# Column sums of cos·Q and sin·Q: from wide TensorE products to elementwise sums on VectorE

## The reference, cut to what matters

```
Q = relu(x @ Wq + bq)
V = x @ Wv + bv
Q = relu(layer_norm(Q))
H = sum(Q, axis=1) ** 2,  scaled by pi / (2 m)          # one angle for each node
cosQ, sinQ = Q * cos(H), Q * sin(H)
out  = cosQ @ (cosQ.T @ V) + sinQ @ (sinQ.T @ V)
norm = cosQ @ sum(cosQ, axis=0) + sinQ @ sum(sinQ, axis=0) + 1e-10
h    = out / norm + gcn(x) + V
result = layernorm(x + relu(layer_norm(h, gamma, beta)))
```

## Time and profile before

| | |
|---|---|
| Time, median of 3 runs | 1686.92 us |
| Profiled execution, its own time | 1702.43 us |
| Its span, first to last instruction | 1700.6 us |
| Mean granted TensorE clock | 0.977 of full speed |
| TensorE matmuls busy | 1529.1 us (90%) |
| VectorE busy | 1093.6 us (64%) |
| GpSimd busy | 916.2 us (54%) |
| ScalarE busy | 608.9 us (36%) |
| DMA moved | 423.89 MB, mean 249 GB/s |

### The profile page before, as it was taken

The page is one execution under the profiler, slowest core; times in us unless marked ns, Lnnn a source line. Parts: engine busy times, 40 slices in busy tenths (PEclk is TensorE's granted clock), DMA queues, the critical chain, the costliest instruction groups (busy, mean ns, idle before and its releaser), DMA issues.

```text
span 1700.6 us, 25340 instructions
## 1 busy us (share of the span) xinstructions
PE 1529.1 (90%) x7913; PEld 943.0 (55%) x7913; DVE 1093.6 (64%) x3318; ACT 608.9 (36%) x1384; POOL 916.2 (54%) x1026
## 2 busy tenths in 40 slices
PE   5788999899999997999998999889999999999994
PEld 3566777666555563443433433336666766666663
DVE  6999676676666666434445444447777768777774
ACT  5999875533233222111112111113333333333332
POOL 0000000166666766666676777666666666666662
PEclk9999999999999997999999999989999999999997
DMA  6444444598888888888888888879888888888884
GB/s 224 139 154 160 151 157 153 201 314 291 297 285 286 290 287 263 262 266 267 266 253 257 264 270 273 271 208 288 283 271 279 277 271 277 286 273 271 285 256 142
DMA packets 172759, 423.89 MB, mean 249 GB/s; under 512 B 24142, under 2 KB 25802, under 8 KB 172616
## 3 DMA queue, kind: packets, MB, share of 16 engines
q0 software_dynamic: 71120, 236.74, 45.5%
q1 hardware_dynamic: 79980, 146.16, 25.1%
q10 hardware_dynamic: 21516, 39.29, 6.1%
HBM read 351.42 MB, written 70.67 MB: 248 GB/s over the span
## 4 chain that ended last, share of the span: by engine, by line
PE 60%; issue 12%; DVE 10%; DMA 7%; POOL 4%; ACT 4%; another core or an unknown queue 1%; POOLq 0%; SPq 0%; DVEq 0%; ACTq 0%
PE bank L1382 13%; PE bank L1383 12%; PE bank L1384 12%; PE bank L1503 10%; PE bank L1505 9%; POOL gathered L566 4%; DMA gathered<-scaled_g,index_slots 3%; DVE stage L984 3%; DVE stage L980 2%; ACT stage L638 1%; DMA scaled_g<-pairs 1%; DVE operands L993 1%; ACT operands L617 1%; DMA combine<-values 1%
## 5 line engine op out<-in xcount | busy, mean ns | idle before, releaser
L566 POOL DMA_INDIRECT gathered<-scaled_g,index_slots x882 | 877.1, 994 | 418.1 <-issue 203.8
L1100 DVE TENSOR_SCALAR one_hot<-iota_bf,dst_in_tile,gathered 128x128 bf16<-128x128 bf16 x882 | 269.7, 327 | 373.8 <-DMA gathered<-scaled_g,index_slots 212.9
L1503 PE MATMUL bank<-gathered,one_hot 128*128 128x512 f16 x882 | 344.9, 391 | 77.0 <-issue 39.4
L1382 PE MATMUL bank<-weights,operands 128*128 128x512 f32 x784 | 398.4, 508 | 14.2 <-DVE stage L1000 4.4
L1505 PE MATMUL bank<-gathered,one_hot 128*128 128x512 f16 x882 | 339.6, 385 | 5.1 <-issue 4.6
L1383 PE MATMUL bank<-weights,operands 128*128 128x512 f32 x784 | 313.7, 400 | 1.8 <-issue 1.8
L1384 PE MATMUL bank<-weights,operands 128*128 128x512 f32 x784 | 312.6, 399 | 0.6 <-issue 0.6
L1503 PEld LDWEIGHTS bank<-gathered,one_hot 128*128 128x128 bf16 x882 | 85.5, 97 | 253.5 <-issue 163.5
L736 ACT ACTIVATE operands_f<-operands,cos_sin_v 128x512 f16<-128x512 f32 x98 | 70.2, 721 | 360.5 <-remote 171.2
L1382 PEld LDWEIGHTS bank<-weights,operands 128*128 128x128 f32 x784 | 150.7, 192 | 80.7 <-issue 7.6
L551 POOL COPY dst_slots<-dst_cols 128x18 f32 x49 | 12.7, 260 | 332.7 <-issue 331.2
(11 more groups left out here) (243 smaller groups left out, 2066.8 us busy)
## 6 DMA issues: line engine op xcount, KB each, us to landing
operands<-values SPq DMA_DIRECT2D x98, 256.0 KB
stage<-in_x SPq DMA_DIRECT2D x96, 256.0 KB, 2.7
turned_x<-operands SPq DMA_DIRECT2D x37, 512.0 KB, 3.3
operands<-turned_x SPq DMA_DIRECT2D x37, 512.0 KB
gathered<-scaled_g,index_slots POOLq DMA_INDIRECT x882
scaled_g<-pairs SPq DMA_DIRECT2D x49, 260.0 KB, 2.0
pairs<-scaled_g SPq DMA_DIRECT2D x49, 260.0 KB
values<-stage ACTq DMA_DIRECT2D x49, 256.0 KB
```

What stands on the lines that cost most here:

```text
L566: pool.indirect_dma_start(out=plain(row_ring[k % RING]), out_offset=None, in_=table, in_offset=bass.IndirectOffsetOnAxis(ap=index_slots[:, ...
L1100: dve.tensor_scalar(one_hot[:, k % HOT, :], iota_bf[:, :], column(dst_in_tile, seq % 2 * PER_TILE + k), scale_of(row), ALU.is_equal, ALU.m ...
L1382: pe.matmul(out_ap, a_hi, b_hi, start=start and n == 0, stop=False, skip_group_check=True)
L1503: pe.matmul(gcn_banks[seq % 2][:, :], one_hot[:, k % HOT, :], hi, start=k == 0, stop=False, skip_group_check=True)
```

## The change

TensorE's two wide products of each tile are taken out, with `cs_wide`, its high and low parts, and the product that cleared bank 7. In their place VectorE keeps two 128 x 512 float32 rooms, `angle_sums`, in two buffers of `pairs` that are free by then. They are zeroed before the cosine sweep, and in each sweep `add_half` does room = half of Q · cosine (or sine) + room for both halves of each tile: 98 instructions in the cosine sweep, and 98 in the sine sweep. At the end of each sweep TensorE turns the room into four columns with four small fp32 products against a column of ones (`turn_sums(sweep)`), and `split_sums(sweep)` makes four of the eight numbers at a time. So the sine sums come at the end of the sine sweep, and no longer at that of the cosine sweep.

```diff
-                act.activation(cs[:, :, 0:2], ..., ACT.Copy, scale=UP).then_inc(s["cs_rounded"], 1)
-                act.wait_ge(s["cs_split"], 1)
+                act.wait_ge(s["angles_scaled"], 1)
...
             def split_angles():
-                dve.wait_ge(s["cs_rounded"], 1)
-                dve.tensor_tensor(both_parts[:, :], ident[0:4, 0:2], ident[0:4, 2:4], ALU.add)
-                dve.tensor_scalar(cos_sin_v[:, :], cos_sin[:, :], v_factor, None, ALU.mult)
-                dve.scalar_tensor_tensor(cs[:, :, 2:4], pair, UP, cs[:, :, 0:2], ALU.mult, ALU.subtract)\
-                    .then_inc(s["cs_split"], 1)
+                dve.wait_ge(s["cos_sin_ready"], 1)
+                dve.tensor_scalar(cos_sin_v[:, :], cos_sin[:, :], v_factor, None, ALU.mult).then_inc(s["angles_scaled"], 1)
+                for room in angle_sums:
+                    dve.memset(room, 0.0).then_inc(s["sums_begun"], 1)
+
+            def add_half(sweep, t, half):
+                g, r, room = 2 * (sweep * TILES + t) + half, rows_of(t), angle_sums[sweep]
+                dve.wait_ge(s["sums_begun"], 2)
+                dve.wait_ge(s["sums_added"], g)
+                dve.scalar_tensor_tensor(room[0:r], halves(q_tile(t))[half][0:r], column(cos_sin, 2 * t + sweep)[0:r],
+                                         room[0:r], ALU.mult, ALU.add).then_inc(s["sums_added"], 1)
...
-            def split_sums():
+            def split_sums(sweep):
+                mine = moment_sums[:, 4 * sweep:4 * sweep + 4]
...
                 for t, at in in_flight(cos_at, TILES, q):        # VectorE
                     if at == 1:
                         m_split(2 + t)
+                    if at in (1, 2):
+                        add_half(0, t, at - 1)
...
-                if q == COS_END + 3:
-                    keep_sums()
                 if q == COS_END + 7:
-                    split_sums()
+                    split_sums(0)
...
+                    if at in (0, 2):                             # VectorE, sine sweep
+                        add_half(1, t, at // 2)
                 if q == SIN_END:
+                    split_sums(1)
                     take_sines(0)
                     take_sines(1)
...
-                    if sweep == 0 and b == 0:                    # TensorE, m_products
-                        pe.matmul(banks[7][:, :], angles, f[0], start=False, stop=False, ...)
-                    if sweep == 0 and b == 1:
-                        pe.matmul(banks[7][:, :], angles, f[1], start=False, stop=False, ...)
...
-            def turn_sums():
-                pe.wait_ge(s["sums_kept"], 1)
+            def turn_sums(sweep):
+                pe.wait_ge(s["sums_added"], 2 * TILES * (sweep + 1))
                 for b in range(B):
-                    last = pe.matmul(banks[2][:, 2 * b:2 * b + 2], sum_rows[:, b * P:(b + 1) * P], both_parts[:, :], ...)
+                    last = pe.matmul(sum_banks[sweep][:, b:b + 1], angle_sums[sweep][:, b * P:(b + 1) * P],
+                                     ones_column[:, :], start=True, stop=True)
...
-                if q == COS_END + 5:                             # TensorE
-                    turn_sums()
+                if q == COS_END + 3:
+                    turn_sums(0)
...
                 if q == SIN_END:
+                    turn_sums(1)
                     o_turn(0, 0)
```

More of the change, by code:

```diff
@@ L135, in build_layer @@
         sums = sb("sums", [P, B, 4], F32R)
-        cs_wide = sb("cs_wide", [P, 4 * (TILES - 1) + P], F16)
-        cs = cs_wide[:, 0:4 * TILES].rearrange("p (t c) -> p t c", c=4)
-        both_parts = sb("both_parts", [4, 2], F32)
+        ones_column = sb("ones_column", [P, 1], F32)
         bn_parts = sb("bn_parts", [P, 3, 6], F32)
@@ L146, in build_layer @@
         edge_banks = banks[6], banks[7], banks[0], banks[6]
-        sum_rows = pairs[0:4, 3, 0:D]
+        angle_sums = [pairs[:, 1 + sweep, 0:D] for sweep in range(2)]
+        sum_banks = banks[2], banks[7]
         turned_banks = banks[2], banks[7]
@@ L253, in build_layer @@
             "extra_ready", "gcn_summed", "v_summed", "spread_step", "extremes_turned",
[L254 removed]
+            "factor_spread", "o_split", "o_normed", "o_root1", "o_stats2",
             "o_root2", "variance_linked", "factors_linked", "norm_linked", "mix_linked",
@@ L846, in _ @@
             dve.reg_mov(extras_done, 0)
-            dve.memset(cs_wide[:, 4 * TILES:], 0.0)
+            dve.memset(ones_column[:, :], 1.0)
             dve.memset(ln_eps, LN_EPS).then_inc(s["ident_ready"], 1)
@@ L1194, in take_cosines @@
                 dve.tensor_copy(stage[:, 2 + b, :], banks[3 + b][:, :]).then_inc(s["cos_taken"], 1)
-            def keep_sums():
-                dve.tensor_copy(sum_rows, banks[7][0:4, :]).then_inc(s["sums_kept"], 1)
-            def split_sums():
+            def split_sums(sweep):
+                mine = moment_sums[:, 4 * sweep:4 * sweep + 4]
                 dve.wait_ge(s["rows_bias_loaded"], 32)
[L1201 to L1206, removed]
+                dve.wait_ge(s["sums_turned"], sweep + 1)
+                link(dve.tensor_scalar(mine, sum_banks[sweep][:, 0:4], 1.0 / (UP * UP), None, ALU.mult))
+                link(dve.tensor_copy(sums[:, :, sweep], mine))
+                link(dve.tensor_tensor(sums[:, :, 2 + sweep], mine, plain(sums[:, :, sweep]), ALU.subtract))
+                link(dve.tensor_scalar(mine, mine, moment_up, None, ALU.mult))
             def fix_cosines(b):
@@ L1210, in fix_cosines @@
                 dve.wait_ge(s["cos_taken_act"], 2)
-                dve.scalar_tensor_tensor(stage[:, 2 + b, :], bias[:, 1, :], moment_sums[:, 2 * b:2 * b + 1],
+                dve.scalar_tensor_tensor(stage[:, 2 + b, :], bias[:, 1, :], moment_sums[:, b:b + 1],
                                          stage[:, 2 + b, :], ALU.mult, ALU.add).then_inc(s["moment_fixed"], 1)
@@ L1216, in take_sines @@
                 dve.wait_ge(s["moment_split"], 4)
-                dve.scalar_tensor_tensor(stage[:, 2 + b, :], bias[:, 1, :], moment_sums[:, 2 * b + 1:2 * b + 2],
+                dve.scalar_tensor_tensor(stage[:, 2 + b, :], bias[:, 1, :], moment_sums[:, 4 + b:5 + b],
                                          banks[3 + b][:, :], ALU.mult, ALU.add).then_inc(s["moment_fixed"], 1)
@@ L1585, in m_begin @@
                     pe.wait_ge(s["late_paired"], done(FUSED - 1))
-                    pe.wait_ge(s["cs_split"], 1)
                 pe.wait_ge(s["m_split"], done(sweep * TILES))
-                if sweep == 0:
-                    pe.matmul(banks[7][:, :], zero_bf[:, :], m_parts(0)[0], start=True, stop=False,
-                              skip_group_check=True)
                 for b in range(B):
```

13 lines of the change are left out of this document (2 added, 11 removed).

## The result

The changed kernel takes 1692.76 us (median of 11 runs, 1690.16 to 1697.95); the kernel before took 1687.30 us beside it (11 runs, 1683.31 to 1691.98). The ratio is 1.0035, 95% interval [1.0021, 1.0049]: slower by 5.9 us, 3.5 to 8.3 (0.35% of 1687.30 us). The forecast was 1698 us, with a range of its own of 1692 to 1706, and a loss of 11.3 us. So the direction holds, the size is about half, and the time lies at the lower edge of that range.

What follows compares the result with a forecast made beforehand. The prediction took the supply of gathers, mostly GpSimd's own time, to bound the kernel. Its terms, -2.3 + 1 + 10.6 + 2 = +11.3 us on 1686.9 us, gave 1698 us, own range 1692 to 1706, overall 1674 to 1716.

Steps and rivals of the forecast that it cites:

- Products taken out: Cosine sweep: 98 products, 21.1 us of TensorE, go; only the share tied to waits for a buffer counts, -2.3 us.
- One-hots that come later: Both sweeps: VectorE's added sums delay its one-hots without making it the bound, +1 us.
- Longer gathers: Both sweeps: sums reading two SBUF tiles lengthen gathers, 0.086 us each in cosine, 0.131 in sine, 21.2 us of GpSimd.
- Half of it reaches the end: Both sweeps: half of the 21.2 us is absorbed in waits for a buffer, the rest lengthens the kernel, +10.6 us.
- End of the sine sweep: Sine sweep's end: turning the room and four small VectorE operations ahead of `take_sines` cost 1 to 4 us, taken as +2 us.
- the one in which TensorE was the bound: Rival: TensorE set the cosine sweep's pace, so 10.7 us come off in all, 1676 us; chance 0.20.
- the one of the late one-hots: Rival: VectorE's one-hots come too late in the sweeps, 19 us and 2 us at the end, 1708 us; chance 0.13.
- all is absorbed: Rival: buffer waits in the sweeps swallow the longer gathers, the other terms cancel, 1687 us; chance 0.27.
- the long gathers behind the starts of `add_half`: Sign, both sweeps: mean gather rises to 1.03 us and more, the long ones following starts of the added sums.
- the unchanged cosine sweep: Sign that the forecast is right: the cosine sweep stays near 233 us.
- TensorE below 85% in it: Sign that the forecast is right: matmuls of the cosine stretch fall below 85% of its time.
- the sine sweep should have grown by 6 us or more: Sign that the forecast is right: the sine sweep becomes longer by at least 6 us.

Runs made afterwards that it cites:

- no_adds: The changed kernel without its 196 sums on VectorE, wide products still removed; 1703.31 us, ratio 0.9999 to the kernel before.
- early_turn: As no_adds, with both rooms turned and split at the end of the cosine sweep; 1702.54 us, ratio 0.9988 to the kernel before.
- light_sweeps: As no_adds, with a third of the products of both sweeps also left out; 1587.23 us, ratio 0.9973 to the kernel before.
- psum_sums_beside_products: Kernel before with the 196 sums added beside its wide products, room in a PSUM bank, so one SBUF input each; 1590.74 us, ratio 0.9993.
- adds_beside_again: Kernel before with the 196 sums of two SBUF inputs added beside its wide products, on a 1592 us chip; 1623.75 us, ratio 1.0199.
- adds_beside_products: Kernel before with the 196 sums of two SBUF inputs added beside its wide products, on the 1703.48 us chip; 1711.17 us, ratio 1.0052.
- one_input_elsewhere: Kernel before without the change, five wide VectorE operations of each tile rewritten to read one SBUF tile and one PSUM bank; 1592.11 us, ratio 1.0000.
- psum_rooms: Changed kernel with its rooms in PSUM, so each sum reads one SBUF tile; 1706.70 us, ratio 1.0014 to the kernel before.
- changed_third: The changed kernel as it is, measured again on a chip where the kernel before takes about 1592 us; 1620.61 us, ratio 1.0184.

## Why the prediction was right, and where its sizes were off

**Products taken out, -2.3 us: nothing speaks against it.** no_adds shows -0.2 us (-3.2 to +2.9) with the new end of the sine sweep in it, early_turn -2.0 us (-4.8 to +0.9) without. The reading that TensorE at 93% is still not the bound of the cosine sweep, taken from the equal pace of the two sweeps in the earlier trace rows, was confirmed most strongly by light_sweeps.

**One-hots that come later, +1 us: right within the interval.** psum_sums_beside_products has -1.1 us (-3.5 to +1.4) for 196 operations, on a chip of 1592 us.

**Longer gathers, 21.2 us of GpSimd: right in kind, too small by a third.** The run shows 31.4 us, 0.16 us for each of the 196 sums and not 0.086 and 0.131. The term that was mis-sized is the price of one operation, taken from the groups of before. There 52 gathers start in the 98 operations of `m_split` (L1189), with 0.33 us of the operation still to come on average, and each takes 0.195 us more than the median: 0.10 us for each operation. In the changed kernel 98 gathers start in the 196 sums, which is about as often, but with 0.47 us still to come, and each takes 0.303 us more: 0.15 us for each sum. So not the chance of a meeting was wrong, but how early in the operation it comes. Why gathers start earlier in a sum than in `m_split` is not shown. The Trainium skill, page "SBUF — State Buffer", sections "Who interferes with whom" and "Summary: rules for kernel authors", with its rule that the second of the two is held until the first has finished, gave an estimate of 37.6 us, 6.2 too many where the rows gave 10.2 too few. Its condition, two SBUF inputs, is what the pair psum_sums_beside_products and adds_beside_again shows to be decisive. The trace agrees one way only: a gather is held by a sum, but a sum that starts during a gather is not (0.744 us against 0.745).

**Half of it reaches the end, +10.6 us: this is the term that was off.** On the chips measured the share differs. With adds_beside_products it is 8.9 us of (1.032 - 0.994) x 882 = 33.5 us, a quarter. In the run of the change itself the loss is 5.9 of 31.4 us, a fifth. On the chips of 1592 us all of it comes through: 30.0 us of time for 27.1 us of issuing, with the idle time unchanged at 292.9 us. "Half" was a guess between 0 and 1, for which the prediction gave a reason but no row that sizes it.

**End of the sine sweep, +2 us: not separated.** The bound of 4 us supposed that the signal of the small products comes late; it did (7.77 us of waiting), and most of it was hidden as supposed. no_adds against early_turn gives 1.9 us within a larger uncertainty. In the traces nothing of it is left later on: from the 531st gather to the 701st it is 260.1 us in the changed kernel and 260.4 before.

**The sum.** With the products at -2 us and the end at +2 us, the 5.9 us measured are nearly all longer gathers, a fifth of the 31.4 us. Two errors partly cancelled: the gathers grew by 31.4 and not 21.2 us, and a fifth and not half of it arrived. That the time fell into the range was also luck of the chip: where the kernel before takes 1592 us, the same change costs 28.7 us, more than twice the forecast and outside the 5 to 19 us of its range. Of the rivals, the one in which TensorE was the bound and the one of the late one-hots are refuted; "all is absorbed" is refuted too, but on the first chip it was nearer than the forecast's share of one half. Of the signs named beforehand, the long gathers behind the starts of `add_half`, the unchanged cosine sweep and TensorE below 85% in it came true; the sine sweep should have grown by 6 us or more and grew by 2.0 us between the same gathers, or 3.5 us by its pace (0.024 us in 147 steps). One sum of the prediction doesn't come out: 1708 us and half of the longer gathers, 10.6 us, are 1718.6 us, not 1716.

## What to carry to other kernels

A busy share of 90% doesn't name the bound: compare the pace of the one thing that every step needs, here the gather, between stretches that load the busy engine differently. Where GpSimd issues the DMAs that set this pace, count the VectorE operations with two wide SBUF inputs as GpSimd's work too, and give one of the inputs to a PSUM bank where one is free: the same 196 sums cost 33 us or nothing on the faster chips. one_input_elsewhere is the warning beside it: shorter gathers alone gained nothing there. What a kernel waits out in one execution is not a reserve that can be spent on every chip: this change costs 5.9 us on a slow one and 28.7 us, five times as much, on a fast one.

## What the runs showed of the hardware that was not expected

The kernel before takes 1687, 1703, 1592 and 1592 us in four comparisons, each with its changed kernels in step. The traces of the two kinds differ in one view above all, the waits. On the chips of 1687 and 1703 us many waits end "remote", by no recorded instruction: ahead of the gathers 41.9 us in the kernel before over its span (9.5 of it in the cosine sweep), 44.0 in no_adds, 24.6 in adds_beside_products. On the chips of 1592 us none of the traces has a single wait of that kind. On the former, a signal of TensorE can also come late: at the end of the sine sweep of the changed kernel its small products are recorded until 1130.7 us, and VectorE goes on at 1138.5; in no_adds and psum_rooms VectorE waits 5.91 and 5.48 us at the same place. In changed_third, where the products are recorded until 1096.9 us, VectorE does the same operation without a wait:

```profile
1096.24 0.74 DVE L1127 SCALAR_TENSOR_TENSOR combine<-bank,dinv,combine 128x512 f32<-128x512 f32 x1
1097.03 0.16 DVE L1203 TENSOR_SCALAR moment_sums<-bank 128x4 f32<-128x4 f32 x1
```

If such late signals hold the gathers back whatever GpSimd does, the longer gathers would be absorbed there and not on the other chips, as measured. That is argued and not shown: no run changes the signals alone. Why the signals are late on some chips stays open.
